# Experts' layer of a decoder block as one stream of token tiles

## What is computed

```python
rw = _gating(hidden_states, sim_matrix, gates)       # routing weights, tokens x 16
q = jnp.einsum('bte,bted->btd', rw, jnp.einsum('btc,ecd->bted', hidden_states, q_proj))
k = ...   # the same with k_proj
v = ...   # the same with v_proj
scores = jnp.einsum('bqd,bkd->bqk', q, k) * scale    # heads of 64, causal mask
attn = jnp.einsum('bqk,bkd->bqd', jax.nn.softmax(scores, axis=-1), v)
mixed = attn[:, :, None, :] * rw[..., None]
return jnp.einsum('bted,edc->btc', mixed, o_proj)
```

## Time and profile before

| | us |
|---|---|
| median of 3 runs | 4721.47 (4720.66 to 4730.45) |
| profiled execution | 4720.34 |
| its span | 4718.5 |
| mean granted TensorE clock | 0.943 of full speed |
| TensorE busy | 4197.2, 89% |
| VectorE busy | 2688.8, 57% |
| ScalarE busy | 1609.3, 34% |
| GpSimd busy | 1397.8, 30% |

### The profile page before, as it was taken

The page is one execution under the profiler, slowest core; times in us unless marked ns, Lnnn a source line. Parts: engine busy times, 40 slices in busy tenths (PEclk is TensorE's granted clock), DMA queues, the critical chain, the costliest instruction groups (busy, mean ns, idle before and its releaser), DMA issues. The chain is left out here.

```text
span 4718.5 us, 62570 instructions
## 1 busy us (share of the span) xinstructions
PE 4197.2 (89%) x21356; PEld 2425.0 (51%) x21356; DVE 2688.8 (57%) x3648; ACT 1609.3 (34%) x2897; POOL 1397.8 (30%) x800
## 2 busy tenths in 40 slices
PE   5899899989999984899989989998996699999997
PEld 3443643554364433543644364446443476767686
DVE  2564465446445633575567466745773766667585
ACT  1354254335524541244234424432443212020202
POOL 1223222312322221376257535752662000000000
PEclk8999899989999997899989999999998899999898
DMA  2221322142123205212422241234111301010100
GB/s 85 65 63 51 83 61 52 48 104 50 45 68 90 48 21 175 63 41 73 133 65 58 90 127 40 68 99 112 41 28 51 112 19 37 18 37 18 37 1 18
DMA packets 120954, 294.62 MB, mean 62 GB/s; under 512 B 18544, under 2 KB 20464, under 8 KB 120624
## 3 DMA queue, kind: packets, MB, share of 16 engines
q1 hardware_dynamic: 110128, 273.06, 21.3%
q10 hardware_dynamic: 10496, 17.31, 1.0%
HBM read 145.87 MB, written 43.25 MB: 40 GB/s over the span
## 5 line engine op out<-in xcount | busy, mean ns | idle before, releaser
L1100 ACT ACTIVATE probs<-half 128x512 f32<-128x512 f32 x2048 | 1112.8, 595 | 1017.3 <-PE half L904 468.1
L901 PE MATMUL half<-stack 97*128 97x512 f32 x2048 | 877.5, 492 | 65.3 <-ACT probs L1100 27.9
L1331 DVE TENSOR_REDUCE mx<-wide 128x1 f32<-128x1024 f32 x512 | 601.8, 1220 | 560.5 <-PE wide L862 554.3
L1327 DVE CUSTOM_DVE_ANT_0 wide<-wide,mask_q 128x1024 f32<-128x1024 f32 x512 | 617.5, 1247 | 280.4 <-PE wide L862 262.8
L862 PE MATMUL wide<-stack 96*128 96x512 f32 x2048 | 652.2, 434 | 90.5 <-DVE mx L1331 39.2
L901 PEld LDWEIGHTS half<-stack 97*128 97x128 f32 x2048 | 374.8, 194 | 679.5 <-ACT probs L1100 318.2
L766 POOL TENSOR_TENSOR psums<-psums,probs 128x1024 f32<-128x1024 f32 x232 | 550.1, 2391 | 158.8 <-ACT probs L1100 139.5
L845 PE MATMUL acc<-probs,v 128*32 128x512 f32 x4096 | 554.5, 612 | 3.1 <-ACT u L1069 3.0
L1675 PE MATMUL work_e<-w_in_e,x_e 128*128 128x512 f32 x2304 | 524.0, 389 | 0.0
L862 PEld LDWEIGHTS wide<-stack 96*128 96x128 f32 x2048 | 389.0, 197 | 214.8 <-DVE mx L1327 66.2
L1675 PEld LDWEIGHTS work_e<-w_in_e,x_e 128*128 128x128 f32 x2304 | 431.9, 188 | 90.6 <-DVE weighted_e L1969 1.0
(11 more groups left out here) (247 smaller groups left out, 4381.3 us busy)
## 6 DMA issues: line engine op xcount, KB each, us to landing
stack<-qk SPq DMA_DIRECT2D x336, 256.0 KB, 4.9
y<-x SPq DMA_DIRECT2D x8, 2048.0 KB, 8.5
x<-y SPq DMA_DIRECT2D x8, 2048.0 KB, 7.8
x_t<-xts ACTq DMA_DIRECT2D x16, 1024.0 KB, 5.6
mstage<-mask SPq DMA_DIRECT2D x32, 512.0 KB, 4.1
mstage<-mask_t SPq DMA_DIRECT2D x32, 512.0 KB, 3.9
stage<-x_t SPq DMA_DIRECT2D x24, 512.0 KB, 3.6
stack<-first SPq DMA_DIRECT2D x48, 256.0 KB, 5.0
```

The costliest lines, as they stand in the source:

```text
L901: last = pe.matmul(bank[:, :], stack[0:3 * DH + 1, s, 2 + h, kt * P:(kt + 1) * P], stack[0:3 * DH + 1, s, h, c * CH:(c + 1) * CH], start=T ...
L1100: act.activation(probs[:, kt % 2 * 2 + h, c * CH:(c + 1) * CH], bank[:, :], ACT.Exp, scale=SCALE).then_inc(free, 1)
L1327: dve.tensor_tensor_reduce(bank[:, :], bank[:, :], mask_q[:, t, :], 1.0, -3e38, ALU.add, ALU.max, mx[:, p % 3, n:n + 1]).then_inc(free, 1)
L1331: dve.tensor_reduce(mx[:, p % 3, n:n + 1], bank[:, :], AX.X, ALU.max).then_inc(free, 1)
```

## The change

Tiles of all batches form one stream. In a slot g TensorE makes the six projection banks of tile g, the attention of tile g-1 and the output of tile g-2, across batch borders; `token_slot` writes the order of a slot and `token_sections` three lists, an opening of two slots, a body of eight slots that a loop runs three times, and a closing list of eight (six with projections). Further:

- logits are made per tile, tokens on partitions at once (12 matmuls of 16 columns); the sum of squares comes from ScalarE (`Square` with an accumulator); the routing of tile g+1 is a step of slot g, between the fourth and the fifth bank;
- VectorE only multiplies the projection banks; GpSimd folds the sixteen experts with four additions (512, 256, 128, 64 columns); it also makes the low part of x, and normalises the output;
- the norm's root and its five small VectorE operations are made per tile;
- dividing by the sum and spreading is one VectorE operation;
- x and the residual are loaded, and the output stored, a tile at a time; weights pass a staging tile of two buffers and their chunks lie between the steps of the opening.

```diff
+def token_slot(g, tile):
+
+    two, one, now, nxt, after = (tile(n) for n in range(g - 2, g + 3))
+    keys = key_halves(one[1]) if one else ()
+    order = [
+        ("load", after), ("split", nxt), ("square", nxt),
+        ("p", now, 0), ("turn", one), ("out", two), ("p", now, 1),
+        *[("score", one, c) for c in keys],
+        ("lg", nxt), ("norm_root", nxt), ("var_root", two), ("p", now, 2), ("ln", two), ("p", now, 3),
+        *[("prob_t", one, c) for c in keys],
+        ("route", nxt), ("p", now, 4), ("pv", one), ("store", two), ("p", now, 5), ("mixed_t", one, 0), ("mixed_t", one, 1),
+    ]
+    return [step for step in order if step[1]]
...
+    for step in token_slot(0, opening) + token_slot(1, opening):
+        if step[0] == "p" and step[1] == (1, 0) and step[2]:
+            first += [("w", 2 * step[2]), ("w", 2 * step[2] + 1)]
+        if step[0] == "p" and step[1] == (1, 1) and step[2] < 4:
+            first.append(("w", 12 + step[2]))
+        first.append(step)
+    body = [step for g in range(2, TT + 2) for step in token_slot(g, inner)]
...
+                        for n in (CH, CH // 2, CH // 4):
+                            pool.tensor_tensor(buf[:, 0:n], buf[:, 0:n], buf[:, n:2 * n], ALU.add)
+                            pool.drain()
+                        dst = qk[:, t % 2, w // 2, :] if w < 4 else v[:, t, :]
+                        pool.tensor_tensor(dst, buf[:, 0:HD], buf[:, HD:2 * HD], ALU.add)
+                        pool.drain().then_inc(summed, 1)
...
                     elif kind == "mixed_t":
-                        _, qt, g = step
-                        pe.wait_ge(mixed_ready, i * TT + qt + 1)
+                        g = step[2]
+                        pe.wait_ge(mixed_ready, number + 1)
...
+                    elif kind == "square":
+                        act.wait_ge(y_in[t % 2], (number + (2 - t % 2)) * 8)
+                        alone(act)
+                        act.activation(junk[:, :], y[:, t, :], ACT.Square, accum_out=sums[:, t:t + 1])
+                        act.drain().then_inc(squared, 1)
...
+                    elif kind == "route":
+                        act.wait_ge(pick_in, number + 1)
+                        alone(act)
+                        act.activation(pick[:, :], pick[:, :], ACT.Exp)
+                        act.drain().then_inc(pick_out, 1)
...
+            def route(sec, step, number, t):
+
+                dve.wait_ge(rooted, number + 1)
+                alone(dve)
+                better_root(small[:, 1:2], sums[:, t:t + 1], root[:, t:t + 1], small[:, 2:3])
+                dve.reciprocal(small[:, 1:2], small[:, 1:2])
+                bank, free = full(dve, sec, ("lg", step[1]))
...
+                dve.tensor_scalar(pick[:, :], lg[:, :], small[:, 3:4], None, ALU.subtract)
+                dve.drain().then_inc(pick_in, 1)
...
+                dve.wait_ge(pick_out, number + 1)
...
-                        dve.tensor_scalar(attn[:, :], bank[:, 0:HD], rtot[:, qt:qt + 1], None, ALU.mult)\
-                           .then_inc(free, 1)
-                        dve.drain()
-                        dve.tensor_tensor(mixed[:, :, :], attn[:, :].unsqueeze(1).to_broadcast([P, E, HD]),
-                                          rw[:, qt, :].unsqueeze(2).to_broadcast([P, E, HD]), ALU.mult)
+                        dve.scalar_tensor_tensor(out=mixed[:, :, :],
+                                                 in0=bank[:, 0:HD].unsqueeze(1).to_broadcast([P, E, HD]), scalar=over,
+                                                 in1=rw[:, t, :].unsqueeze(2).to_broadcast([P, E, HD]),
+                                                 op0=ALU.mult, op1=ALU.mult).then_inc(free, 1)
```

More of the change, by code:

```diff
@@ new lines, in token_sections @@
+def token_sections():
+    opening = lambda n: (1, n) if n >= 0 else None
+    inner = lambda n: (n // TT, n % TT)
+    closing = lambda n: (0, n) if n < TT else None
+    first = [("load", (1, 0)), ("w", 0), ("w", 1), ("load", (1, 1)), ("split", (1, 0)), ("square", (1, 0)),
+             ("lg", (1, 0)), ("norm_root", (1, 0)), ("route", (1, 0))]
+    for step in token_slot(0, opening) + token_slot(1, opening):
[5 more added lines that the diff above has]
+    body = [step for g in range(2, TT + 2) for step in token_slot(g, inner)]
+    body += [("pad", n) for n in range(-sum(step[0] in BANK_KINDS for step in body) % RING)]
+    return first, body, [step for g in range(2, TT + 2) for step in token_slot(g, closing)]
@@ L1453, in expert_layer @@
 def expert_layer(nc, io):
-    steps = ffn_steps()
-    PER = len(steps) // RING
-    use_no = {s: n for n, s in enumerate(steps)}
+    lists = [list(steps) for steps in token_sections()]
+    ring = Ring(lists, BANK_KINDS, RING)
     ctx = ExitStack()
@@ L1845, in _ @@
+                        bank, free = full(act, sec, step)
+                        alone(act)
+                        act.activation(mixed_t[:, 0, g * 4:g * 4 + 4, :].rearrange("p k n -> p (k n)"), bank[:, :], ACT.Copy)
+                        act.drain().then_inc(hi_ready, 1)
+            run(Section(0, None, False, True, lists[0]))
+            with act.Fori(0, B - 1) as i:
+                run(Section(1, i, True, True, lists[1]))
+            run(Section(2, None, True, False, lists[2]))
         @block.vector
@@ L1867, in better_root @@
                 dve.drain()
-                dve.tensor_tensor(hold, hold, root, ALU.add)
+                dve.tensor_tensor(hold, hold, root_, ALU.add)
                 dve.drain()
@@ new lines, in run @@
+            def run(sec):
+                for step in sec.steps:
+                    kind = step[0]
+                    if kind == "w":
+                        n = step[1]
+                        w = w_chunks[n]
+                        dve.wait_ge(w_hi, n + 1)
+                        dve.tensor_tensor(w[:, 1, :, :], w_stage[:, n % WS, :, :], w[:, 0, :, :].bitcast(F32),
+                                          ALU.subtract).then_inc(stage_free, 1)
+                        dve.drain().then_inc(w_ready, 1)
+                        continue
+                    if kind == "pad":
+                        continue
+                    tile = step[1]
+                    t = tile[1]
+                    number = token_tile(sec, tile)
+                    if kind == "route":
+                        route(sec, step, number, t)
+                    elif kind == "p":
+                        w = step[2]
+                        bank, free = full(dve, sec, step)
+                        alone(dve)
+                        if w % 2 == 0 and (sec.number or 3 * t + w // 2 >= 2):
+                            dve.wait_ge(summed, number * 3 + (w // 2 - 1))
+                            alone(dve)
+                        prod = weighted[:, (3 * t + w // 2) % 2, w % 2 * CH:(w % 2 + 1) * CH]
@@ L2006, in _ @@
+                        alone(dve)
+                        last_c = key_halves(t)[-1]
+                        dve.wait_ge(prob_ready, score_no(sec, tile, last_c) + 1)
+                        alone(dve)
+                        over = rtot[:, t % 2:t % 2 + 1]
+                        if last_c:
+                            dve.tensor_tensor(over, total[:, t % 2, 0:1], total[:, t % 2, 1:2], ALU.add)
                             dve.drain()
-                            dve.reciprocal(rtot[:, qt:qt + 1], rtot[:, qt:qt + 1])
+                            dve.reciprocal(over, over)
@@ L2065, in constants @@
+            run(Section(0, None, False, True, lists[0]))
+            with dve.Fori(0, B - 1) as i:
+                run(Section(1, i, True, True, lists[1]))
+            run(Section(2, None, True, False, lists[2]))
 def constants():
```

721 lines of the change are left out of this document (317 added, 404 removed).

## The result

The changed kernel took **4891.62 us** (median of 4 runs, 4890.93 to 4893.21) beside 4721.07 us for the kernel before on the same chip. The ratio is 1.036, 95% interval [1.034, 1.038]: slower by 170 us. Its profiled execution took 4891.83 us, span 4889.8, mean granted clock 0.928 where it was 0.943. The forecast was 4845 us with a range of 4765 to 4930.

What follows compares the result with a forecast made beforehand. Projections already ran at TensorE's own rate; in the new slot TensorE would wait for VectorE's chain. Terms 97 + 29 x 35.2 + 29 + 36 = 1182.8 us against 1058.5, +124, gave 4845 us, range 4765 to 4930.

Steps and rivals of the forecast that it cites:

- opening: First two slots, with set-up, five pairs of weight chunks and two routings: 97 us, bounds 85 and 110.
- 29 slots with routing: Steady stream: each slot 27.8 of TensorE's work, 6.1 of stand and 1.3 of clock, 35.2 us.
- slot without routing: Last slot of the steady stream, no next tile to route: 28 us with a little wait, 29.
- tail: Last two slots: the old 24.8 us, an output tile 5.55 and scores to mixed tile 6.5, 36 us.
- TensorE's work in a slot: Projections, output, transposes, scores, values and logits of one slot together: 27.8 us.
- VectorE's chain and the stand: Fourth bank's end to the mixing, 13.4 us with routing 8.5; TensorE has 7.3 meanwhile, so stands 6.1 each slot.
- The clock: TensorE's granted clock falls after each stand: 1.3 us a slot, bounds 0 and 1.8.
- The range: Low end: slot 32.5, 4767 us; high end: slot 38, 4927 us; given as 4765 to 4930.
- A: Rival: VectorE's chain fits beside banks five and six, slot 27.8 to 31, 4680 us, faster; chance 0.08.
- B: Rival: the stand is as forecast but the clock does not fall, slot 33.9, 4808 us; chance 0.15.
- C: Rival: ScalarE idles behind table loads or PSUM products double beside GpSimd, chain 1.4 us longer, 4886 us; chance 0.10.

Runs made afterwards that it cites:

- Experiment 1: Changed kernel with the next tile's routing moved behind the mixed tile's transposes and the logits behind the product with the values; 4650.97 us, ratio 0.985 to the kernel before.
- Experiment 3: Changed kernel with 24 more unused matmuls per slot before TensorE's wait for the mixed tile; 4837.85 us, ratio 1.023 to the kernel before.
- Experiment 7: Late routing (Experiment 1) with four staging buffers for the weights instead of two; 4657.83 us, ratio 0.987 to the kernel before.
- experiment 8: Experiment 7 with the opening's weight pairs one step earlier and the last two tiles normalised by VectorE; 4631.97 us, ratio 0.981 to the kernel before.
- experiment 4: Changed kernel with GpSimd's folds of the keys, in the loop's slots, held until after VectorE's comparisons; 4881.27 us, ratio 1.033 to the kernel before.
- experiment 5: Changed kernel with the expert sums back on VectorE and no folds on GpSimd; 4965.25 us, ratio 1.052 to the kernel before.

## Why the forecast held, and where its terms were off

The experts' layer by the forecast's own terms, in us:

| term | forecast | measured |
|---|---|---|
| opening, to the first mixed tile's transposes (3771.34) | 97 | 111.3 |
| 29 slots with routing | 29 x 35.2 = 1020.8 | 29 x 35.97 = 1043.0 |
| slot without routing | 29 | 28.6 |
| tail (from 4842.98) | 36 | 46.8 |
| sum | 1182.8 | 1229.8 |

**TensorE's work in a slot,** 27.8: held. Experiment 1, with TensorE busy 97%, has slots of 28.23, loop turns among them; twelve 16-column matmuls took 1.50 where 1.6 was taken.

**VectorE's chain and the stand,** 13.4 and 6.1: held. In the slot shown the chain is 13.4 us, from the end of the fourth bank at 4224.67 to the transposes at 4238.10, and the stands are 6.0 in the mean. Experiment 1 shows it as the cause, and that it turns the sign: of the 7.74 us that its slot is shorter, 5.4 are waits of TensorE and 2.4 its busy time. Inside it GpSimd cost 0.7: the comparison 0.74 for 0.42, the multiplication 0.71 for 0.43, the second comparison 0.49 for 0.42. 0.4 was taken, the bound of 0.8 held it. The forecast took for a slowing what is a lock, and the earlier trace rows already show the lock: GpSimd's squares end at 3955.74, VectorE's subtraction needs 1.22 alone, and it ends at 3956.82, about where it would if it began only then.

**The clock,** 1.3 of bounds 0 and 1.8: mis-sized. Experiment 3 gave back 2.11 a slot, above the upper bound. The price came from a single output tile after a 3.4 us stand; after 5.9 us the low level held through the transposes and part of the bank. The 0.8 between 1.3 and 2.1 makes 23 us over 29 slots; that line of the table is off by 22.

**The opening,** 97: mis-sized by 14. The pair was built of landing, copy and subtraction, 7.7 us, with TensorE's bank beside it. The bank is in the ring, and at the low clock. Timeline of PE, kernel after:

```profile
3692.82 5.18 PE L1704 MATMUL work_e<-w_in_e,x_e 128*128 128x512 f32 x12 [7.90 <-DVEq L1961]
...
3702.51 5.44 PE L1704 MATMUL work_e<-w_in_e,x_e 128*128 128x512 f32 x12 [3.27 <-DVEq L1961]
3711.39 4.50 PE L1704 MATMUL work_e<-w_in_e,x_e 128*128 128x512 f32 x12 [3.44 <-DVEq L1961]
3728.77 4.36 PE L1704 MATMUL work_e<-w_in_e,x_e 128*128 128x512 f32 x12 [12.88 <-DVEq L1961]
```

Two turns took 9.3 us on average, and then one 17.4, because the second routing did not lie "beside one of these" but between two of them, in VectorE's list. The five pairs took 47 us (3689.3 to 3736.6) where 38.5 were forecast, and the second slot 35 where 30 were. In experiment 1, where the second routing no longer stands there, the opening is 8 us shorter. Experiment 7 excludes the staging buffers as the bound, experiment 8 shows the ring.

**The tail,** 36: mis-sized by 11. The way from scores to mixed tile was taken from the first tile of a batch, 6.5 us, which has one key tile. The last has eight: two score blocks, two table loads, 16 matmuls by the values. It takes 17.2 us (4851.87 to 4869.03), 10.7 more than forecast. The steps ahead of it took 8.9 us, where an output tile of 5.55 was taken, and those behind it 20.8 for 24.8.

**The range.** Its ends do not follow from the parts named for them. A chain 1.1 shorter and no clock fall make a slot of 32.8, not 32.5, and 4776 us. Logits, clock and GpSimd at their far bounds add 2.0 to 35.2, so 37.2, not 38, and 4903 us. The measured 4891.6 lies inside these narrower ends too, but by 12 us only. All three misses, opening, clock and tail, went the same way.

**Rivals.** A, routing hidden, was refuted for the change as written, and its number, a slot of 28 to 31, is that of experiment 1. The forecast asked whether the chain is short enough, and it is not; it did not ask whether the chain fits once it stands elsewhere in the list. B, no fall of the clock: refuted by the transposes' 1.97 us. C, a dearer hand-over: the exponential started 0.02 us behind the load again, and PSUM products kept 0.692 us; both halves refuted. The Trainium skill's 1.38 us of drain behind a load ("ScalarE: Activation LUTs", section "What ACT_TABLE_LOAD costs") is in no run here.

## What to carry to other kernels

When a batch's work becomes a stream of tiles, ask for each step on a side engine which step of TensorE's list stands behind its result, and put long chains directly after the hand-over TensorE needs, not ahead of it: the same instructions gave +3.6% in one order and -1.5% in the other. Draw the ring before you buy buffers: staging buffers did nothing until the step that closed the ring was moved; then four were worth 8 us against two. And take a term's price from a row in the same state as its place, with the clock after a stand of that length and the tile with as many keys.

## What was unexpected in the hardware

- VectorE and GpSimd at SBUF exclude each other for whole instructions: a 128x16 operation took 1.10 us, its end 0.03 us after the end of GpSimd's fold (experiment 4). A reduction of 256 columns beside the folds kept its 0.42 us, and products from PSUM their 0.69.
- GpSimd's folds hold VectorE, its normalising does not: in experiment 5 thirty sums of two SBUF tiles (128x64) started beside GpSimd's 2.08 us of normalising, and all kept their 0.23 us. Why the two differ no run shows.
- GpSimd's subtract and multiply with two values per partition took 2.08 us for 128x512, where VectorE needs 0.54 to 0.55. GpSimd's 128x512 sum of two tiles took 1.28 to 1.29.
- Giving TensorE 24 more matmuls in every slot, 5.6 us whose result nothing uses, made the kernel 54 us faster.
